# A hand-timed attention kernel: 128 columns for the down projection, a later turn of the rows, half of a feed-forward moved into the last norm

## The reference

```python
# adapter, one expert per sequence
hidden = gelu(x @ down_W.T + down_b)               # 256 -> 64
hidden = (hidden @ W[idx].T + b[idx]) + emb[idx]   # 64 -> 64
x = layernorm(hidden @ up_W.T + up_b + x) * gamma + beta
# transformer layer, conditioned on a timestep
scale, shift = split(silu(sin_emb(t)) @ W_ada + b_ada)
x = layernorm(x) * (1 + scale) + shift
q, k, v = x @ Wq + bq, x @ Wk + bk, x @ Wv + bv    # 16 heads of 16
p = softmax(where(mask, -inf, q @ k.T / 4 + bias)) # bias: 8 x 16 x 512 x 512
x = x + (p @ v) @ Wo + bo
ff = gelu2((layernorm(x) * g2 + beta2) @ W1 + b1) @ W2 + b2   # 256 -> 1024 -> 256
out = x + ff
```

## Time and profile before

| | |
|---|---|
| median of 3 runs | 959.73 us (959.16 to 959.91) |
| profiled execution, its own time | 960.01 us |
| its span, first to last instruction | 958.2 us |
| PE busy in the span | 890.0 us (93%), 6472 matmul instructions |
| DVE, ACT, POOL busy | 703.1, 703.9, 702.8 us (73% each) |
| mean granted TensorE clock | 0.973 of full |
| DMA | 207.41 MB, 71.9% of 16 engines' span on the main queue |

### The profile page before, as it was taken

One profiled execution on the slowest core, in us unless ns is written; L12 is line 12 of the kernel. 1 busy time (PEld: TensorE's weight loads), 2 busy tenths in 40 slices (PEclk: granted clock), 3 DMA queues, 4 the chain that ended last, 5 costly groups with the idle time before them and its releaser, 6 DMA issues. The chain is left out here.

```text
span 958.2 us, 20699 instructions
## 1 busy us (share of the span) xinstructions
PE 890.0 (93%) x6472; PEld 659.6 (69%) x6472; DVE 703.1 (73%) x1901; ACT 703.9 (73%) x1667; POOL 702.8 (73%) x407
## 2 busy tenths in 40 slices
PE   3746889999999999999999999999999999999987
PEld 1425565777777776787777776787777777677765
DVE  4645787878778787878778787888778787675742
ACT  2435888978788787978788787978788787867641
POOL 1417997889788886978688886979788887885700
PEclk7877999999999999999999999999999999999998
DMA  5299969876897769776897769776897669765300
GB/s 158 79 263 335 293 221 256 241 237 200 254 290 206 230 210 255 238 238 198 249 291 209 231 208 270 228 238 200 245 267 214 220 195 274 238 192 166 100 12 11
DMA packets 147950, 207.41 MB, mean 216 GB/s; under 512 B 14385, under 2 KB 62322, under 8 KB 147842
## 3 DMA queue, kind: packets, MB, share of 16 engines
q1 hardware_dynamic: 145474, 204.12, 71.9%
q10 hardware_dynamic: 2368, 1.97, 0.8%
HBM read 185.05 MB, written 20.99 MB: 215 GB/s over the span
## 5 line engine op out<-in xcount | busy, mean ns | idle before, releaser
L492 POOL TENSOR_TENSOR bias_s<-mask_f,bias_s 128x1024 f32<-128x1024 f32 x256 | 601.2, 2372 | 132.5 <-DMA bias_s<-in_bias 132.2
L1371 DVE CUSTOM_DVE_ANT_0 bias_s<-sc,bias_s 128x512 f32<-128x512 f32 x512 | 347.6, 684 | 175.7 <-PE sc L823 165.3
L996 ACT ACTIVATE bias_s<-bias_s,mx 128x512 f32<-128x512 f32 x512 | 371.2, 725 | 91.4 <-DVE mx L1371 89.3
L830 PE MATMUL tp<-ident,bias_s 128*128 128x128 f32 x2048 | 311.5, 275 | 6.4 <-ACT pT L1002 3.4
L830 PEld LDWEIGHTS tp<-ident,bias_s 128*128 128x128 f32 x2048 | 252.1, 142 | 88.9 <-issue 15.0
L1002 ACT COPY pT<-tp 128x512 f32<-128x512 f32 x335 | 194.9, 582 | 100.6 <-PE tp L830 98.1
L823 PE MATMUL sc<-stk,stq 128*128 128x512 bf16 x512 | 196.4, 384 | 24.9 <-DVE mx L1371 14.2
L752 PE MATMUL la<-w_s,act_s 128*128 128x256 f32 x512 | 128.2, 380 | 0.2 <-DVE act_s L1328 0.2
L788 PE MATMUL pv<-pT,v_all 128*32 128x256 f32 x2048 | 124.3, 383 | 0.0
L1378 DVE COPY pT<-tp 128x512 f32<-128x512 f32 x177 | 121.1, 684 | 3.7 <-PE tp L830 3.6
L737 PE MATMUL lc<-hT,w_s 128*128 128x256 f32 x464 | 121.2, 385 | 2.5 <-ACT hT L951 1.9
(11 more groups left out here) (175 smaller groups left out, 797.1 us busy)
## 6 DMA issues: line engine op xcount, KB each, us to landing
bias_s<-in_bias SPq DMA_DIRECT2D x256, 512.0 KB, 4.6
stk<-k_parts SPq DMA_DIRECT2D x128, 96.0 KB, 3.9
stq<-q_parts SPq DMA_DIRECT2D x126, 96.0 KB, 4.1
k_parts<-kb SPq DMA_DIRECT2D x32, 192.0 KB, 2.3
q_parts<-qb SPq DMA_DIRECT2D x30, 192.0 KB, 2.4
xT<-in_x_t SPq DMA_DIRECT2D x8, 512.0 KB, 7.2
k_parts<-kb SPq DMA_DIRECT2D x32, 128.0 KB, 2.3
stk<-k_parts SPq DMA_DIRECT2D x64, 64.0 KB, 4.3
```

The costliest lines, as they stand in the source:

```text
L492: pool.tensor_tensor(tile, mask_f[:, :, :], tile, ALU.subtract).then_inc(s["masked"], 1)
L830: last = pe.transpose(tp[n % 2][:, kt * P:(kt + 1) * P], bias_s[:, n // 2 % NB, n % 2, kt * P:(kt + 1) * P], ident[:, :])
L996: act.activation(tile, tile, ACT.Exp, bias=mx[:, t:t + 1], scale=-1.0, accum_out=sums[:, j, head_of(hh):head_of(hh) + 1]).then_inc(s["prob ...
L1371: dve.tensor_tensor_reduce(out=tile, in0=sc[t % 2][:, :], in1=tile, scale=1.0, scalar=BIG, op0=ALU.add, op1=ALU.min, accum_out=mx[:, t:t + ...
```

## The change

The down projection's weight tile is widened from 64 to 128 columns; GpSimd writes zeros to the 64 new ones at the start, and its matmul then writes all 128 partitions of the bank `lc`, of which the lower 64 are read as before. The transposes of the norm's rows move on TensorE from 12.6 to 13.3, and their copy on ScalarE from 14.0 to 14.6. For chunk 14 (the feed-forward `NCH - 2`, whose times count from iteration 15), W2's steps 1, 2 and 3 move from 27.0, 28.0, 29.0 to 27.6, 28.6, 30.3, steps 4 to 7 from 29.3, 29.6, 30.3, 31.3 to 42.3, 42.6, 43.0, 43.3, which is 10.3 to 11.3 of iteration 16; its sum and its store follow there at 12.3 and 13.0.

```diff
-PE_AT = dict(up=0.3, v=(1.0, 2.0), q=(8.6, 10.0), xt1=12.6, k=(15.6, 16.3), down=(24.3, 25.3),
+PE_AT = dict(up=0.3, v=(1.0, 2.0), q=(8.6, 10.0), xt1=13.3, k=(15.6, 16.3), down=(24.3, 25.3),
              pv=(13.6, 21.6, 29.6, 5.6), spread=(22.3, 6.3))
-ACT_AT = dict(q=(11.0, 12.3), widen=(18.3, 2.3), spread=(23.6, 7.0), k=(17.0, 18.0), xT1=14.0, gelu=26.6)
+ACT_AT = dict(q=(11.0, 12.3), widen=(18.3, 2.3), spread=(23.6, 7.0), k=(17.0, 18.0), xT1=14.6, gelu=26.6)
...
     if f == NCH - 2:
         i = f + 1
         at = dict(hT=18.3, w1=(19.0, 20.0, 20.3, 21.0, 24.0, 24.6, 25.0, 26.0), tanh=(21.3, 22.3, 25.6, 27.3),
-                  gate=(22.3, 23.3, 26.3, 28.0), w2=(26.6, 27.0, 28.0, 29.0, 29.3, 29.6, 30.3, 31.3), out=32.3,
-                  store=33.0)
+                  gate=(22.3, 23.3, 26.3, 28.0), w2=(26.6, 27.6, 28.6, 30.3, 42.3, 42.6, 43.0, 43.3), out=44.3,
+                  store=45.0)
...
-        down_w = sb("down_w", [P, CT, A])
+        down_w = sb("down_w", [P, CT, P])
...
-            load("down_in", [(down_w[:, :, :], downT.rearrange("(c p) a -> p c a", p=P))])
+            load("down_in", [(down_w[:, :, 0:A], downT.rearrange("(c p) a -> p c a", p=P))])
...
+            link(pool.memset(down_w[:, :, A:P], 0.0))
             link(pool.memset(powc[:, :], -0.5))
...
-                last = pe.matmul(lc[0:A, :], down_w[:, ct, :], xT[:, ct, :], start=(ct == 0), stop=(ct == CT - 1))
+                last = pe.matmul(lc[:, :], down_w[:, ct, :], xT[:, ct, :], start=(ct == 0), stop=(ct == CT - 1))
...
             pe.wait_ge(s["down_in"], 16)
+            pe.wait_ge(s["pool_chain"], 1)
             adapter_down(0, 0)
...
                 if c == 0:
-                    dve.wait_ge(s["pool_chain"], 3)
+                    dve.wait_ge(s["pool_chain"], 4)
```

## The result

The changed kernel is slower: 969.61 us in the median (966.1 to 973.9, 8 runs) against 960.28 us for the kernel before beside it (959.2 to 963.1, 8 runs), ratio 1.0094 with a 95% interval of 1.0066 to 1.0121. The forecast was 965.6 us and slower, its range ended at 969.5 us. Against the 959.73 us that it started from, the forecast is a ratio of 1.0061 and the range's end one of 1.0102. The measured ratio lies inside the range, but its interval leaves the forecast itself out, and the plain median is 0.1 us beyond the range's end. The profiled execution took 973.33 us, span 971.2 us; it is one of the slower of the eight.

What follows compares the result with a forecast made beforehand. TensorE was taken to bound iterations 2 to 13. Turn and copy +13.9, iterations 0 and 1 +0.6, width -3.2, end -5.4 gave +5.9 us on 960.01, 965.9, so 965.6 us against the median; range 961.0 to 969.5 us.

Steps and rivals of the forecast that it cites:

- The bound: Iterations 2 to 13: a microsecond TensorE loses or gains is one of the kernel, if VectorE and ScalarE deliver in time.
- Turn at 13.3: Norm rows' transposes on TensorE behind score 13: wait passes to score 13 behind find 11, 0.30 us saved per iteration.
- Copy at 14.6: ScalarE's copy behind soften 14: keys wait 1.36 us, restart costs 0.10 us, price 1.46 us per iteration.
- The faster rival: Copy at 14.6 still comes in time, only gains left: 947.5 us; deciding wait at the keys 0.87 us; chance 0.13.
- Iterations 0 and 1: Same two moves there: 0 in iteration 0, where POOL sets the pace, +0.6 us in iteration 1; bounds 0 and 2.4.
- Width: Down projection with 128 columns: 0.29 us seam saved per step, 0.3 us for iteration 1's two, -3.2 us in all.
- The rival that the width is not the cause: Down projection: the width of 64 does not make the seam, so no gain: 968.8 us; chance 0.07.
- the rule of the Trainium skill: Down projection: loads run under matmuls only where row groups differ; both widths use all rows, which would give 968.8 us.
- The end: Chunk 14's W2 into the last norm: `wo` 3.1 us earlier, 2.3 us by the clock staying up, -5.4 us.
- The rival of the falling clock: Last norm: the clock falls all the same, 2.3 us come back: 967.9 us; chance 0.10.
- The whole: Whole kernel: +13.9 + 0.6 - 3.2 - 5.4 = +5.9 us, forecast 965.6 us; slower 0.79, same 0.08, faster 0.13.

Runs made afterwards that it cites:

- experiment 6: The kernel before with only the copy on ScalarE moved to 14.6, the turn left at 12.6: 979.70 us, ratio 1.0197.
- experiment 3: The kernel before with only the new times of chunk 14's W2, sum and store: 954.97 us, ratio 0.9927.
- experiments 4: The kernel before with only the turn moved to 13.3 and the copy to 14.6: 976.50 us, ratio 1.0145.
- experiment 1: The changed kernel with the copy on ScalarE back at 14.0: 948.13 us, ratio to the kernel before 0.9848.
- experiment 2: The kernel before with only the 128 weight columns in the down projection, their load, zeros, matmul and waits: 958.89 us, ratio 0.9979.
- experiments 1 to 8: Eight follow-up kernels with parts of the change alone or combined, or with the copy back, `weigh` or `xm` moved: medians from 947.48 to 979.70 us.

## Why the prediction was right, point by point

- **The bound.** Right. In iterations 2 to 13 the parts add up to hundredths: -0.26 (width), -0.29 (turn), +1.42 (copy) make +0.87 us, and the changed kernel has +0.86 us. Nothing that these times resolve is left for another engine.
- **Turn at 13.3.** Predicted 0.30 us saved, measured 0.29. The wait went where it was said to go, to score 13 behind find 11.
- **Copy at 14.6.** Predicted 1.46 us, measured 1.42 (experiment 6), which is the 1.32 us lost in starts and the 0.10 us of the slower restart. The chain score 14, find 14, soften 14, copy stands in the trace as it was worked out, except that the copy starts a tenth before the row of the accumulator ends (692.25 against 692.35). The faster rival fell: its break-even was a wait of 0.87 us, the wait is 1.32 us.
- **Iterations 0 and 1.** From the keys of iteration 1 to those of 2 the forecast had +0.9 us (1.16, less 0.3 for the width), and the traces show it as sharply as the later ones: 54.62 us before, 55.64 in both profiles of the changed kernel, so +1.0 us; 54.32 with the turn alone, 55.95 with the copy alone. What lies between the keys of iteration 0 and those of 1 can't be told from noise: 46.1 us before, 47.7 and 46.1 in the changed kernel, 45.5 to 46.7 in the kernels without the copy's move. The keys of iterations 0 and 1 both wait 1.16 us in the changed kernel, against 0.17 us before, so the wait is there in iteration 0 too. Whether it costs nothing in iteration 0 and 0.6 us in iteration 1, as forecast, stays open.
- **Width.** Predicted 0.29 us per down step, measured 0.28. The rival that the width is not the cause fell, and with it the rule of the Trainium skill (TensorE: Matmul & The Clock Gate, Part 3) quoted there: with 65, 96 and 128 columns the weights fill all rows as with 64, and the matmuls follow without a seam. But the reason is the step from 64 to 65 columns and not the filling of the array, which the prediction did not separate. The loads' own added time (190 against 136 ns) left no trace in the sum. The 0.3 us forecast for the two steps of iteration 1 did not come: from the keys of iteration 1 to those of 2 the width alone takes 54.63 us, the kernel before 54.62 us.
- **The end.** Predicted 5.4 us, measured 5.4 (experiment 3, with 3.2 us up to `wo` for 3.1 and 2.2 us by the clock for 2.3). The rival of the falling clock fell.
- **The whole.** From the keys of iteration 2 to the end the terms give 11 x 1.16 - 2.9 - 5.4 = +4.5 us, the two profiles of the changed kernel +4.1 us (769.0 against 764.9). The measured +9.3 us are 3.4 us more than the forecast, and 5.2 of them lie before that point. There the sum had 0.6 + 1.16 - 0.3 = +1.5 us, with nothing for the time before the loop: that is what it had too small. That the ratio still fell inside the range is in part luck, since the range's upper end was made of a width without gain and a falling clock, and neither came true.
- **The start, how far it is known.** The eight runs lie in two groups, 966.1 to 967.7 us, near the forecast, and 971.5 to 973.9 us. Two profiles, one of the upper group and a later one of 966.70 us, differ only before the keys of iteration 2, most of it by the rate of TensorE before the loop. If the rest is as constant in every run as in these two, each run's span gives its own start. By this estimate the keys of iteration 2 begin at 195.3 to 202.8 us in the eight runs, median 198.3 us; in the kernel before at 190.5 to 199.0 us, medians 194.7 and 193.5 us in its 17 and its 18 runs. The kernels of experiments 4 and 6, which have the copy's move, reach them at 197.3 and 196.6 us in the median (five and six runs), the kernels without it at 192.9 to 195.2 us; with the move and the later weigh it is 195.0 us. So the wider matmuls and the added wait at the start are unlikely causes: experiment 1 has both, with 192.9 us in four runs, and experiment 2 has both, with 195.2 us in twelve. A part can be the price of the copy's move in iterations 0 and 1. By the same estimate four of the eight runs reach these keys after 200 us, and of all runs of the other kernels in experiments 1 to 8 only one does; that is not explained. The kernel before, too, spreads over 8 us (957.3 to 965.5 in 17 runs); the range should have allowed for this, which the three runs shown then (959.2 to 959.9) did not let see.

## What to carry to other kernels

In a schedule of in-order engines, a copy has a time only in name: what counts is the instruction it stands behind, and what that one waits for. Before a step is moved past another engine's work, follow the waits of what it is moved behind up to the engine that is the bound; here two thirds of a slot meant a whole chain of score, maximum and exponential. And when a kernel is bound by one engine, cut the traces at the same instruction of two iterations: the mean between them was the same to 0.01 us in two profiles of the changed kernel whose whole times differ by 6.6 us.

## What the hardware showed that I had not expected

- A float32 down step of 512 columns costs 0.28 us more with 64 weight columns than with 65, 96 or 128 (an iteration with such steps on average 53.67 against 53.41, 53.41 and 53.42 us).
- The time up to the loop's first keys varies from one execution to the next: the keys of iteration 0 start between 90.9 and 98.8 us in thirteen profiles, the latest in the one whose matmuls from 31 to 42 us ran at half the rate throughout.
- In that profile the clock column of the windows of 5 us says 1.00 up to 45 us although the matmuls from 31 to 42 us are at half the rate. In the start the distance from matmul to matmul is the safer reading:

```profile
30.00:35.00 5.00, 5.00 (x12) 2.35 (x11) 3.70 (x11) 0.00 (x0) 0.00 (x0) 1.00 0.07 21
```
